# State scan of a four-layer stack: where the phases lie, who rounds them and who takes the fraction

## What is computed

```python
phi = k_val[..., None] * theta                    # b, l, K, H, M
re_k, im_k = jnp.cos(phi), jnp.sin(phi)
den = jnp.cumsum(p_w[..., 0], axis=1)
num_re = jnp.cumsum(pwb * re_k, axis=1)
num_im = jnp.cumsum(pwb * im_k, axis=1)
inv = lax.rsqrt(jnp.maximum(den, 0.0001)); inv = (inv * inv)[..., None, None]
s_re, s_im = num_re * inv, num_im * inv
out_re = jnp.sum(s_re * qr + s_im * qi, axis=-1)
out_im = jnp.sum(s_im * qr - s_re * qi, axis=-1)
y_re = out_re * norm_scale[:H] * jnp.diagonal(W_re)
y_im = out_im * norm_scale[H:] * jnp.diagonal(W_im)
y = jax.nn.silu((y_re + y_im).reshape(b, l, DIM_K))
```

## Time and profile before

| | us |
|---|---|
| median of 3 runs | 8536.2 |
| lowest and highest | 8526.68, 8543.41 |
| the profiled execution, its own time | 8548.21 |
| its span | 8546.5 |
| mean granted clock of TensorE over it | 0.906 of full |

### The profile page before, as it was taken

One profiled execution on the slowest core, in us unless ns is written; L12 is line 12 of the kernel. 1 busy time (PEld: TensorE's weight loads), 2 busy tenths in 40 slices (PEclk: granted clock), 3 DMA queues, 4 the chain that ended last, 5 costly groups with the idle time before them and its releaser, 6 DMA issues. The chain is left out here.

```text
span 8546.5 us, 122867 instructions
## 1 busy us (share of the span) xinstructions
PE 6867.6 (80%) x30852; PEld 3464.3 (41%) x30852; DVE 4888.6 (57%) x12027; ACT 2745.7 (32%) x6011; POOL 1567.3 (18%) x843
## 2 busy tenths in 40 slices
PE   6799878988898866998994487777895788888978
PEld 2233345644454432222222353334443455444544
DVE  3555467533763435777775749984335664237634
ACT  0255525422461101555551103321110254114611
POOL 1100124100510012000000008860001441005100
PEclk9899989999999987999997699988898899899989
DMA  5322245522453164222223221113001355224531
GB/s 174 93 60 59 47 148 160 191 67 68 149 180 116 52 239 135 72 60 67 62 48 101 86 83 26 29 38 94 30 27 56 118 162 179 66 65 150 164 126 47
DMA packets 919478, 832.72 MB, mean 97 GB/s; under 512 B 237352, under 2 KB 784129, under 8 KB 918849
## 3 DMA queue, kind: packets, MB, share of 16 engines
q1 hardware_dynamic: 489520, 505.60, 20.5%
q10 hardware_dynamic: 429568, 323.08, 12.1%
HBM read 485.98 MB, written 345.74 MB: 97 GB/s over the span
## 5 line engine op out<-in xcount | busy, mean ns | idle before, releaser
L1216 ACT ACTIVATE Catt_E<-Catt_t 128x512 f32<-128x512 f32 x1024 | 577.1, 595 | 505.8 <-DVE Catt_t L1179 320.6
L1155 DVE CUSTOM_DVE_ANT_0 Catt_S<-Catt_s,Catt_win 128x1024 f32<-128x1024 f32 x512 | 621.7, 1216 | 41.8 <-DMA Catt_win<-skewed 39.6
L1155 DVE CUSTOM_DVE_ANT_0 Aatt_S<-Aatt_s,Aatt_win 128x128 f32<-128x128 f32 (+7 forms) x512 | 377.2, 756 | 323.9 <-PE Aatt_s L1094 318.2
L1137 PE MATMUL Catt_o<-Catt_E,Catt_V 128*32 128x256 f32 (+1 forms) x3840 | 550.4, 406 | 0.0
L1216 ACT ACTIVATE Aatt_E<-Aatt_t 128x512 f32<-128x512 f32 (+3 forms) x768 | 355.4, 490 | 323.5 <-PE Aatt_t L1119 258.2
L1179 DVE TENSOR_TENSOR Catt_t<-Catt_t,Catt_near 128x256 f32<-128x256 f32 (+2 forms) x640 | 281.4, 457 | 268.5 <-PE Catt_t L1116 236.9
L1116 PE MATMUL Catt_t<-Catt_Q,Catt_K 123*128 123x512 bf16 x1024 | 329.7, 390 | 93.7 <-ACT Catt_E L1216 71.5
L1094 PE MATMUL Catt_s<-Catt_K,Catt_Q 96*128 96x512 bf16 x1024 | 325.7, 401 | 47.7 <-DMA Catt_near<-near_s 38.0
L2280 PE MATMUL scan_cum<-scan_X,scan_after 128*128 128x512 f32 x448 | 253.2, 649 | 120.2 <-DVE scan_pr L2349 116.0
L1137 PE MATMUL Aatt_o<-Aatt_E,Aatt_V 128*32 128x256 f32 (+2 forms) x2304 | 323.5, 388 | 0.0
L2282 PE MATMUL scan_cum<-scan_X,scan_upto 128*128 128x512 f32 x512 | 280.8, 640 | 38.1 <-POOL scan_X L2256 23.7
(11 more groups left out here) (704 smaller groups left out, 15217.3 us busy)
## 6 DMA issues: line engine op xcount, KB each, us to landing
bias_rows<-line SPq DMA_DIRECT2D x16, 960.0 KB
skewed<-bias_win ACTq DMA_DIRECT2D x16, 960.0 KB, 6.1
Catt_win<-skewed SPq DMA_DIRECT2D x16, 960.0 KB, 4.8
rec<-state_in_r ACTq DMA_DIRECT2D x32, 416.0 KB, 2.4
scan_r<-rec SPq DMA_DIRECT2D x64, 208.0 KB
Aatt_Q<-q_parts SPq DMA_DIRECT2D x32, 384.0 KB
Aatt_K<-k_parts SPq DMA_DIRECT2D x32, 384.0 KB
Catt_Q<-q_parts SPq DMA_DIRECT2D x32, 384.0 KB
```

Source lines behind the costliest of these rows:

```text
L1137: ins = t.matmul(o_ps[f:f + 2 * hd, x:y], V[:, b, kb, h, :], E[:, kb % NB, h, x:y], start=kb == 0, stop=kb == end and y == hi)
L1155: v.tensor_tensor_reduce(out=S[:, j % 2, 0:w], in0=s_ps[j % 2][:, 0:w], in1=win[:, 0 if causal else h, w0:w0 + w], scale=-1.0, scalar=BIG, ...
L1216: a.activation(E[:, kb % NB, h, lo:hi], t_ps[n % 2][:, 0:hi - lo], ACT.Exp, scale=scale).then_inc(exped, 1)
```

## The change

`ph` becomes one buffer in PSUM (2 banks), `ys` two buffers in PSUM (a bank each). ScalarE adds 1.5 x 2^23 to `ph` and writes `nn` (`whole`, Identity with a bias column), and VectorE computes (`nn` - 1.5 x 2^23) - `ph` in one scalar_tensor_tensor, which is the negative of the fraction before; the sine's scale changes its sign. GpSimd no longer has `fraction`, and its `weigh` also waits for VectorE's weighing of the same step. The sine half goes first on TensorE and in `read`; GpSimd's `add` waits for the cosine half's reading. All later parts have one lag more.

```diff
-        ph, f, nn = pl.sb("ph", [P, 2, W]), pl.sb("f", [P, 2, W]), pl.sb("nn", [P, 2, W])
+        f, nn = pl.sb("f", [P, 2, W]), pl.sb("nn", [P, 2, W])
-        ys = pl.sb("ys", [P, 2, P])
-        quarter = pl.sb("quarter", [P, 1])
+        quarter, magic = pl.sb("quarter", [P, 1]), pl.sb("magic", [P, 1])
+        ph = pl.ps("ph", (P, W))
+        ys = [pl.ps(f"ys{i}") for i in range(2)]
 GpSimd
-            def fraction(it, j):
-                n = it * ST + j
-                g.wait_ge(ph_done, n + 1)
-                g.wait_ge(trig_done, n + 1)
-                g.tensor_tensor(f[:, j % 2, :], ph[:, j % 2, :], nn[:, j % 2, :], ALU.subtract).then_inc(f_done, 1)
             def weigh(it, m):
+                g.wait_ge(x_done[1], it * ST + (m + 3))
                 g.wait_ge(trig_done, it * ST + (m + 3))
                 g.wait_ge(c_done[0], it * ST + (m + 1))
...
             def add(it, m):
-                g.wait_ge(c_used[1], it * ST + (m + 2))
+                g.wait_ge(c_used[0], it * ST + (m + 2))
-            pipelined(g, B, ST, ((1, weigh), (0, fraction), (2, add)))
+            pipelined(g, B, ST, ((2, weigh), (3, add)))
 TensorE
-                    for i in range(2):
+                    for i in (1, 0):
 ScalarE
+            def whole(it, j):
+                n = it * ST + j
+                a.wait_ge(ph_done, n + 1)
+                a.wait_ge(f_done, n + 1)
+                a.activation(nn[:, j % 2, :], ph[:], ACT.Identity, bias=magic[:]).then_inc(rounded, 1)
-                a.activation(sn[:, s, :], f[:, s, :], ACT.Sin, scale=TWO_PI)
+                a.activation(sn[:, s, :], f[:, s, :], ACT.Sin, scale=-TWO_PI)
-            pipelined(a, B, ST, ((0, trig), (3, store)))
+            pipelined(a, B, ST, ((1, trig), (0, whole), (4, store)))
 VectorE
+            def fraction(it, j):
+                n = it * ST + j
+                v.wait_ge(rounded, n + 1)
+                v.wait_ge(trig_done, n + 1)
+                v.scalar_tensor_tensor(out=f[:, j % 2, :], in0=nn[:, j % 2, :], scalar=-MAGIC, in1=ph[:],
+                                       op0=ALU.add, op1=ALU.subtract).then_inc(f_done, 1)
             def phase(it, j):
-                n, g = it * ST + j, j // NT
+                g = j // NT
+                v.drain()
                 v.wait_ge(r_in[j % R], it * (ST // R * 16) + (j // R + 1) * 16)
-                v.wait_ge(f_done, n + 1)
-                v.tensor_tensor(khm(ph[:, j % 2, :]), khm(th[:, g * W:(g + 1) * W]),
+                v.tensor_tensor(khm(ph[:]), khm(th[:, g * W:(g + 1) * W]),
                                 r[:, j % R, 0:P].rearrange("p (k h) -> p k h", k=16).unsqueeze(3).to_broadcast([P, 16, SH, SM]),
-                                ALU.mult)
-                v.drain()
-                v.tensor_scalar(nn[:, j % 2, :], ph[:, j % 2, :], MAGIC, -MAGIC, ALU.add, ALU.add).then_inc(ph_done, 1)
+                                ALU.mult).then_inc(ph_done, 1)
             def read(it, j):
-                for i, dst in enumerate((pr, pi)):
+                for i, dst in ((1, pi), (0, pr)):
             def reduce(it, j):
-                v.tensor_reduce(ys[:, j % 2, :], pr[:, j % 2, :].rearrange("p (e m) -> p e m", m=SM), AX_X, ALU.add)
+                v.tensor_reduce(ys[j % 2][:, 0:P], pr[:, j % 2, :].rearrange("p (e m) -> p e m", m=SM), AX_X, ALU.add)
...
-            pipelined(v, B, ST, ((0, phase), (1, weigh), (2, read), (3, reduce)))
+            pipelined(v, B, ST, ((1, fraction), (0, phase), (2, weigh), (3, read), (4, reduce)))
```

More of the change, by code:

```diff
@@ L2208, in stage_state_scan @@
         ph_done = pl.sem("ph_done")
+        rounded = pl.sem("rounded")
         f_done = pl.sem("f_done")
@@ L2237, in _ @@
             g.memset(quarter[:], float(np.pi / 2))
+            g.memset(magic[:], MAGIC)
             g.drain()
@@ L2242, in _ @@
                             channel_multiplier=1).then_inc(made, 1)
-            g.sem_inc(f_done, 2)
             g.sem_inc(x_done[0], 2)
             g.sem_inc(sum_done, 2)
-            def fraction(it, j):
-                n = it * ST + j
-                g.wait_ge(ph_done, n + 1)
-                g.wait_ge(trig_done, n + 1)
-                g.tensor_tensor(f[:, j % 2, :], ph[:, j % 2, :], nn[:, j % 2, :], ALU.subtract).then_inc(f_done, 1)
             def weigh(it, m):
+                g.wait_ge(x_done[1], it * ST + (m + 3))
                 g.wait_ge(trig_done, it * ST + (m + 3))
@@ L2316, in _ @@
             v.sem_inc(x_done[1], 2)
+            v.sem_inc(f_done, 2)
             for i in range(2):
@@ L2353, in reduce @@
                 v.wait_ge(sum_done, it * ST + (j + 3))
-                v.tensor_reduce(ys[:, j % 2, :], pr[:, j % 2, :].rearrange("p (e m) -> p e m", m=SM), AX_X, ALU.add)
+                v.tensor_reduce(ys[j % 2][:, 0:P], pr[:, j % 2, :].rearrange("p (e m) -> p e m", m=SM), AX_X, ALU.add)
                 v.drain()
                 v.wait_ge(y_out[j % 2], it * (ST // 2 * 16) + (j // 2 + 1) * 16)
-                v.tensor_tensor(y[:, j % 2, :].rearrange("p (k h) -> p k h", k=16), ys[:, j % 2, :].rearrange("p (k h) -> p k h", k=16),
+                v.tensor_tensor(y[:, j % 2, :].rearrange("p (k h) -> p k h", k=16), ys[j % 2][:, 0:P].rearrange("p (k h) -> p k h", k=16),
                                 r[:, j % R, 3 * P + 16:].unsqueeze(2).to_broadcast([P, 16, SH]), ALU.mult).then_inc(y_done, 1)
-            pipelined(v, B, ST, ((0, phase), (1, weigh), (2, read), (3, reduce)))
+            pipelined(v, B, ST, ((1, fraction), (0, phase), (2, weigh), (3, read), (4, reduce)))
 def stage_experts(nc, act_in, router, wg, wu, wd, out):
```

## The result

| | before | changed |
|---|---|---|
| median, us | 8538.1 (4 runs, 8526.7 to 8543.4) | 8420.2 (4 runs, 8418.6 to 8423.6) |
| profiled execution, span, us | 8546.5 | 8418.7 |
| scan stage, first phase to the end of the last `y`, us | 621.3 | 503.7 |

The changed kernel takes 0.9864 of the time, 95% interval 0.9847 to 0.9881: 118 us less. The prediction said 8418. The stage alone is 117.6 us shorter (5120.92 to 5742.19 before, 5112.93 to 5616.57 now); the two spans differ by 10 us more, which lies in stages that are the same code, 8.0 of it before the first phase. In the eleven profiled executions of this study the rest of the program, the same code in all, took 7902 to 7925 us.

The account below looks back on a forecast made before the run. VectorE was taken to bound the scan stage's step, 9.44 us falling to 7.41. Fill 13.5 plus 58 x 2.03, less 10.5 for cold starts and 3 at the end, gave 118 us saved: 8536.2 to 8418, range 8395 to 8465.

Parts of the forecast that it names:

- What GpSimd held: VectorE instructions with two SBUF inputs, or `nn`, exclude GpSimd; each step loses 1.54 us in `nn`, 1.1 in `y`.
- Fraction: Moved to VectorE with one SBUF and one PSUM input: 1.28 us, 1.36 with the drain ahead of phase.
- Phase into PSUM: VectorE's phase writing PSUM instead of SBUF: 0.04 us more, 1.17 to the next start.
- `y`: VectorE's `y`, reading `ys` from PSUM, no longer held by GpSimd's add: 0.29 us long, 0.21 to the next start.
- Step: Phase to phase on VectorE in the scan stage: 7.41 us instead of 9.44, 2.03 less.
- Waits behind first blocks: TensorE idles 3.7 us after each half's first block, then runs at its lower clock: 1.5 us charged seven times, 10.5.
- Fill: Start of the scan stage: sixth phase at 32.4 us instead of 45.85, 13.5 less.
- end: Last phase to last `y`: 30 us for 26.9, 3 more, from one more lag and TensorE's last two steps.
- the clock in ordinary steps: Rival: TensorE's clock keeps falling in ordinary steps, 20 steps at 1.5 us cost 30 instead of 10.5: 8438; chance 0.14.
- The lock: Rival: despite PSUM inputs, `y` and fraction are held by GpSimd's add, 1 us x 64: 8482; chance 0.05.
- The table: Rival: ScalarE's Identity evicts the sine's table, two loads of 1.28 us a step: 8482; chance 0.04.
- The rival that ends slower: TensorE at its lower clock through the stage, 12.9 us a step: 8758; slower under mean clock 0.68; chance 0.02.

Follow-up runs that it names:

- The first two experiments: Two runs, each against the changed kernel: `ys` back in SBUF, 8469.7 us; `ph` in SBUF, 8467.8 us.

## Why the prediction was right

Term by term, by the prediction's own steps:

- **What GpSimd held.** 1.54 us in `nn` and 1.1 in `y` were read as waits for GpSimd, and the rule taken from `pr` and `pi` (two SBUF inputs are held, a PSUM input isn't). The first two experiments move one tile each and switch the wait on and off. This was the step on which the forecast hung, and it is shown for `y` and for the fraction; the wait in `nn` went with the instruction, and no edit tests it by itself.
- **Fraction**: taken as 1.28, measured 1.210. The row of 512 columns that it came from takes 0.750 us, where this one's 1.210 less 512 columns at 1.04 ns would leave 0.68. That row's scalar is a column in SBUF and the fraction's a constant; whether that is the reason, no run says. Fraction to phase 1.30 instead of 1.36.
- **Phase into PSUM**: 0.04 taken, 0.02 measured (1.233 against 1.212), and 0.007 in the experiment that moves it back.
- **`y`**: 0.29 and 0.21 to the next start, both as forecast. By the 62 cycles that the Trainium skill (VectorE: DVE Perf Modes, the cycle table in the section on the errata) charges a PSUM source more, the estimate was 0.36, and it isn't that: 0.291 with its input in PSUM, 0.293 at its shortest with it in SBUF.
- **Step**: 7.41 forecast, 7.34 to 7.46 measured, 7.39 in the mean of the 49 ordinary steps. Most of the 0.12 us between the shortest and the longest appears at the drain (reduce to `y` 1.29 or 1.37), not as a wait for another engine; what sets it stays open.
- **GpSimd over 0.3 us ahead of phase**: 0.36.
- **ScalarE**: whole at 1.114 for 1.15 and never awaited past the fill; no further table load.
- **Waits behind first blocks**: 7 x 1.5 = 10.5 us; measured six long steps of 8.99 to 10.16 us, 12.2 us over 7.4 together, one first block without. Right in cause and nearly in size. Two of the six cost 2.7 rather than 1.7: both `pi` and `pr` waited. Three steps, 7.9 us long, 1.6 us over 7.41 in all, were not foreseen. They lie 16 steps apart, at the turns of the loop over the sequences, and the time shows between `y`, fraction and phase with no other engine waited for; in the kernel before no step there is longer than 9.45.
- **Fill** 31.4 us for 32.4, **end** 29.8 for 30.

So 13.5 + 58 x 2.03 - 10.5 - 3 became 14.5 + 106.0 - 2.9, where 106.0 is all that fell into the body (548.5 us from the sixth to the last phase before, 442.5 now; 107.2 was forecast for it): 118 both times. The stretch from the sixth to the last phase was forecast at 440.3 us (58 x 7.41 + 10.5) and took 442.5: the waits behind first blocks and the three steps at the turns of the loop cost 3.2 more than was charged, and the ordinary steps gave back 1.0. The fraction's 0.06 a step and phase's 0.02 did not come through whole: the reduce with its drain took 1.29 or 1.37 us where 1.28 was taken. In the kernel before it took 1.28 or 1.35 too, and there `y`, held until the add's end, hid the difference. The fill gave 1 us more than forecast. So the mechanism and the terms hold to a few microseconds; that the sum comes out at 118 to the microsecond, and the time within 2 us of 8418, is luck, since the rest of the program alone moves by more than that from one execution to the next.

Of the rivals, the clock in ordinary steps needed pauses, and those shrank to 0.2 to 0.4 us; full steps behind them stayed at 7.1. The lock was as read. The table stayed. The rival that ends slower wanted a granted clock under 0.68; from 5120 to 5600 us it is 0.96.

## What to carry to other kernels

When an instruction's median is far above its minimum, look at what the other engine was doing when it ended; then ask which of its inputs could lie elsewhere, and what stands behind it in the same engine's order. A hold that is removed moves to the next instruction that can be held: count through the whole time that the other engine is busy, and place instructions there that it can't hold. And an engine with idle time may still be one whose start, not whose speed, has to be set.

## What was not expected

- More matmul work made the kernel faster: 32 float32 matmuls with a zero matrix more over the stage (4 in each of 8 first blocks) take 8 to 10 us off it, since TensorE's pause of 3.7 us and the matmuls at the lower clock behind it (pairs of up to 2.08 us for 1.02 to 1.10) go.
- The same pause isn't always followed by the lower clock: at one of the seven first blocks the next pairs took 1.10 and 1.02 us behind a pause of 3.78, and that step was 7.46 us long. It was the fifth of the seven in one execution and the last in the other. The runs don't say what decides it.
- GpSimd's weighing takes 1.904 us with nothing beside it that holds it, under the 1.957 that was its shortest before.
